# A four-layer sequence kernel on one core: the second layer's norm, skip term, convolution and gate products placed at other steps and on other engines

## The reference, cut to what matters

```python
h = _layernorm(x) * scale1 + shift1                  # per sequence, from cond
xz = h @ in_proj_W;  x_, z = split(xz)               # 512 channels each
x_ = silu(causal_conv(x_, conv_w, 4 taps) + conv_b)
xdbl = x_ @ x_proj_W                                 # rank-16 dt, B and C of 32 states
dt = softplus(xdbl[:16] @ dt_proj_W + dt_proj_b)
def step(hst, inp):                                  # over the 64 tokens, for 32 states
    hst = hst * exp(dt_t * A) + dt_t * B_t * x_t
    return hst, (hst * C_t).sum(states)
y = (ys + Dp * x_) * silu(z) @ out_proj_W            # all of this from h: once forwards,
x = x + gate1 * (y_forwards + y_backwards)           # once over the tokens in reverse
x = x + gate2 * (silu(h2 @ w1) * (h2 @ w2)) @ w3      # h2: the second norm; 384 hidden
```

## Time and profile before

| | us |
|---|---|
| median of 3 runs | 4816.87 |
| lowest and highest | 4813.54, 4817.01 |
| the profiled execution's own time | 4812.7 |
| its span | 4810.9 |
| mean granted TensorE clock, share of full | 0.976 |

### The profile page before, as it was taken

One profiled execution on the slowest core, in us unless ns is written; L12 is line 12 of the kernel. 1 busy time (PEld: TensorE's weight loads), 2 busy tenths in 40 slices (PEclk: granted clock), 3 DMA queues, 4 the chain that ended last, 5 costly groups with the idle time before them and its releaser, 6 DMA issues.

```text
span 4810.9 us, 83433 instructions
## 1 busy us (share of the span) xinstructions
PE 4498.8 (94%) x32892; PEld 3735.8 (78%) x32892; DVE 4162.1 (87%) x4023; ACT 4139.1 (86%) x6894; POOL 3991.3 (83%) x1064
## 2 busy tenths in 40 slices
PE   7989989899899998999999999999999999999998
PEld 5447878788778874458888888888888888888886
DVE  6658988999989976659999998999998998998996
ACT  3449899899899974459999999999999999999995
POOL 4429899889889984538999998998988999989995
PEclk8989999999999998999999999999999999999999
DMA  3001111111111111011121211211211211111111
GB/s 122 1 10 50 49 45 50 49 46 45 50 45 49 51 65 38 1 38 50 54 79 49 79 53 49 79 53 49 79 50 50 80 54 63 64 53 59 58 58 36
DMA packets 89813, 252.74 MB, mean 53 GB/s; under 512 B 12224, under 2 KB 25920, under 8 KB 89424
## 3 DMA queue, kind: packets, MB, share of 16 engines
q1 hardware_dynamic: 89424, 247.40, 14.8%
HBM read 243.70 MB, written 3.67 MB: 51 GB/s over the span
## 4 chain that ended last, share of the span: by engine, by line
PE 42%; ACT 29%; POOL 12%; DVE 9%; issue 7%; DVEq 0%; DMA 0%; POOLq 0%; SPq 0%; ACTq 0%
PE psum L895 11%; PE psum L701 9%; ACT weights_c L1399 9%; PE psum L881 8%; POOL work L2099 6%; PE psum L878 6%; ACT weights_c L1414 5%; PE psum L991 5%; ACT work L1399 4%; ACT work L1414 4%; POOL weights_c L2099 4%; DVE work L1764 3%; PE psum L1067 1%; DVE weights_c L1764 1%; ACT L1190 1%
## 5 line engine op out<-in xcount | busy, mean ns | idle before, releaser
L2099 POOL TENSOR_TENSOR work<-work,weights_a 128x2048 f32<-128x2048 f32 x512 | 2330.7, 4572 | 271.8 <-DVE work L1764 271.1
L1764 DVE TENSOR_TENSOR_SCAN work<-weights_c,psum 128x512 f32<-128x512 f32 x1366 | 1571.6, 1202 | 127.4 <-PE psum L881 118.1
L895 PE MATMUL psum<-ident,work 128*128 128x128 f32 x8192 | 1244.9, 276 | 20.2 <-POOL work L2099 19.8
L2099 POOL TENSOR_TENSOR weights_c<-weights_c,weights_a 128x2048 f32<-128x2048 f32 x256 | 1166.8, 4574 | 87.4 <-DVE weights_c L1764 87.0
L1399 ACT ACTIVATE work<-work,decay 128x504 f32<-128x504 f32 x1366 | 963.9, 706 | 63.8 <-DVE work L1764 30.4
L895 PEld LDWEIGHTS psum<-ident,work 128*128 128x128 f32 x8192 | 973.3, 143 | 28.7 <-POOL work L2099 27.8
L881 PE MATMUL psum<-ident,work 128*128 128x128 f32 x5464 | 941.2, 275 | 0.0
L1764 DVE TENSOR_TENSOR_SCAN weights_c<-work,psum 128x512 f32<-128x512 f32 x684 | 794.6, 1202 | 51.6 <-PE psum L881 44.3
L1764 DVE TENSOR_TENSOR_SCAN work<-work,psum 128x512 f32<-128x512 f32 x682 | 791.1, 1201 | 48.6 <-PE psum L881 42.2
L881 PE MATMUL psum<-ident,weights_c 128*128 128x128 f32 x3752 | 697.9, 276 | 0.0
L881 PEld LDWEIGHTS psum<-ident,work 128*128 128x128 f32 x5464 | 675.5, 143 | 0.0
(11 more groups left out here) (173 smaller groups left out, 6546.8 us busy)
## 6 DMA issues: line engine op xcount, KB each, us to landing
weights_a<-c_rows SPq DMA_DIRECT2D x384, 512.0 KB, 3.6
weights_c<-in_L_cond_fwd_in_w SPq DMA_DIRECT2D x8, 512.0 KB, 7.0
weights_c<-in_L_cond_fwd_xproj_w SPq DMA_DIRECT2D x4, 1024.0 KB, 7.7
weights_c<-in_L_cond_bwd_in_w SPq DMA_DIRECT2D x8, 512.0 KB, 5.9
weights_c<-in_L_cond_bwd_xproj_w SPq DMA_DIRECT2D x4, 1024.0 KB, 7.8
x_stream<-in_x_t SPq DMA_DIRECT2D x4, 512.0 KB, 8.7
weights_a<-in_L_cond_w SPq DMA_DIRECT2D x2, 1024.0 KB, 15.0
weights_a<-in_L_cond_W SPq DMA_DIRECT2D x2, 1024.0 KB, 8.3
```

The costliest lines, as they stand in the source:

```text
L895: last = nc.tensor.matmul(PS[:, t, j * P:(j + 1) * P], buf["ring"][s % RING][:, j, t * P:(t + 1) * P], IDENT[:, :], start=begins, stop=((s ...
L1764: v.tensor_tensor_scan(buf["ring"][s % RING][:, j, along], buf["decay"][q % DECAYS][:, along], PS[:, 4 + q % LOOKAHEAD, along], 0.0, ALU.mult,
L2099: g.tensor_tensor(state, state, buf["c"][:, s // 2 % 2, s % 2, :].unsqueeze(1).broadcast_to([P, DC, T]), ALU.mult).then_inc(ss["prod_ready ...
```

## The change

- **Norm.** The first norm of the next block moves from the odd run to the end of the even run before it (`next_mean` at 81, `next_var` at 90 in runs 2 and 4; 63 and 78 in run 0), with its seven operations on DVE, ACT and POOL.
- **Skip.** The odd run's `skip` becomes `later0` and `later1` at the end of the even run's POOL stream, and `add_skip` of an odd run stands at steps 1 to 4 (`skip_steps`).
- **Input and convolution.** `in` starts at step 3 of the odd run: at 3, 14, 25 and 36 in runs 3 and 5, with a `gate` job between each two, and at 3, 12, 22 and 32 in run 1 and in "run -1". The first taps are done by ACT (`tap`: a Copy with a scale from a vector, 512 columns, and one of 8 columns); DVE does the six others one after each of six steps.
- **z.** In the even run the four `z` jobs come ahead of `bc` (39 to 54; in run 0 from step 3), DVE copies them, and their Silu shares one pair of table loads with `silu_x`, which moves from step 25 to 60 (26 in run 0).
- The other jobs move accordingly: `bc` 63, `dt` 68 to 78 in runs 2 and 4 (71 to 81 in run 6), `bc` 49, `up` 55 to 63, `dt` 67 to 77, `down` 80 and 85 in runs 3 and 5. `dt` jobs have a gap of 3 in place of 4. `bt` and `dtx` end at 106 in all.

The core of the diff:

```diff
-        jobs += [("mean", KC, 3 if gated or tail and head else 10)]
+    if tail or r == RUNS - 1:
+        jobs += [("mean", KC, 3 if head else 10)]
+    if 0 <= r < RUNS - 1 and r % 2 == 0:
+        jobs += [(f"z{j}", KC, 3) for j in range(DC - 1)] + ([("var", KC, 3)] if tail else []) + [("z3", KC, 9)]
...
+    if first:
+        for j in range(DC):
+            jobs += [(f"in{j}", KC, 14 if j == DC - 1 else 7)] + ([(f"gate{j}", KC, 3)] if mlp and j < HIDDEN1 else [])
+        jobs += [("bc", DC, 3)]
...
+        jobs += [(f"dt{j}", 1, 3) for j in range(DC)]
+    if prepares1(r):
+        jobs += [("next_mean", KC, 10), ("next_var", KC, 3)]
...
+def prepares1(r):
+
+    return r % 2 == 0 and 0 <= r < RUNS - 2
...
-PIPES = {1: Pipe(32, 2, pipe_jobs1, lambda r: 2 if r % 2 else 12 if r >= 2 else 28),
+PIPES = {1: Pipe(32, 2, pipe_jobs1, lambda r: 3 if r % 2 else 12 if r >= 2 else 3),
...
+def skip_steps(l, r):
+
+    return (1, 2, 3, 4) if l == 1 and r % 2 else (17, 19, 21, 23)
...
+                    made("pool", f"later{j // 2}@{r - 1}" if l == 1 and r % 2 else f"skip{j // 2}@{r}")
...
+                            yield from product(f"in{j}", [by("dve", f"conv{j}_7"), by("act", f"tap{j}")],
+                                               chunk(W1["inp"], j), h, first(lambda: h_made(r)))
+                            if mlp and j < HIDDEN1:
+                                yield from gates(j)
...
+                    def tap(j):
+
+                        weight = VEC[:, VCONV + j * 4 + 3:VCONV + j * 4 + 4]
+                        yield plan.read(f"in{j}", 2)
+                        made("pe", f"in{j}@{r}")
+                        if r >= 0:
+                            act.wait_ge(ss["skip_added"], r + 1)
+                        f(XS1[:, j, :], bank[f"in{j}"], ACT.Copy, scale=weight)
+                        ends = [ap.rearrange("p (b s) -> p b s", s=SEQ)[:, :, SEQ - 1:SEQ]
+                                for ap in (XC1[:, j, :], bank[f"in{j}"])]
+                        f(ends[0], ends[1], ACT.Copy, scale=weight).then_inc(done(f"tap{j}"), 1)
...
+                    if even:
+                        yield max(plan.read("z3", 5), 26)
+                        made("dve", f"z3@{r}")
                         act.wait_ge(ss["skip_added"], r + 1)
+                        tables(SILU)
+                        f(Z1, Z1, ACT.Silu).then_inc(done("silu_z"), 1)
+                        silu_x(XC1)
+                        tables(EXP_LN)
+                        yield from low_rank()
...
+                    for n, i in enumerate((3, 2, 4, 5, 6, 7)):
+                        shift, d = divmod(i, 2)
...
+                        yield plan.read(f"in{j}", 3 + n)
+                        if i == 3:
+                            made("act", f"tap{j}@{r}")
+                        else:
+                            made("dve", f"conv{j}_{3 if i in (2, 5) else i - 2}@{r}")
...
+                            v.tensor_copy(Z1[:, j, :], bank[f"z{j}"]).then_inc(done(f"z{j}"), 1)
...
+                    if prepares1(r):
+                        halfway = norm(r, plan, done, 2, H, r // 2 + 1, f"z3@{r}", None, "next_")
+                        yield next(halfway)
+                        at = next(halfway)
+                    if even:
+                        yield from skip(r + 1, done, "later", (plan.read("dt3", 15), plan.read("dt3", 19)))
+                    if prepares1(r):
+                        yield at
+                        yield from halfway
```

More of the change, by code:

```diff
@@ L117, in pipe_jobs1 @@
 def pipe_jobs1(r):
-    head, tail = r < RUNS - 1, r >= 2 and r % 2 == 0
-    first, gated = r % 2 == 1 and head, r >= 3 and r % 2 == 1 or r == RUNS
-    norms = tail or r % 2 == 1 and r > 0
+    head, tail, first, mlp = r < RUNS - 1, ends1(r), inputs1(r), gated1(r)
     jobs = []
@@ L227, in pipe_steps1 @@
             g += ["soft0", "product0", "soft1", "product1"]
-        if gated:
+        if prepares1(r):
+            a += ["next_square", "next_var", "next_rstd"]
+            v += ["next_mean", "next_normed"]
+            g += ["next_scaled"]
+        if even:
+            g += ["later0", "later1"]
+        if prepares1(r):
+            g += ["next_h"]
+        if mlp:
             v += ["down0", "end0", "down1", "end1"]
-        if 0 <= r and r % 2 == 0 and head:
-            a += [f"z{j}" for j in range(DC)] + ["silu_z"]
         if head:
@@ L786, in up, with gates @@
-                    def up():
+                    def gates(*chunks):
+                        for j in chunks:
+                            yield from product(f"gate{j}", [by("act", f"gate{j}")], chunk(WM1["w1"], j), h2,
+                                               first(lambda: made("pool", f"h@{r if r == RUNS else r - 1}")))
+                    if tails:
+                        yield from tail(r, product, turn, by, YT1(r), W1["out"])
+                    if tails or r == RUNS - 1:
+                        yield from mean(r, product, by, nb, first(lambda: made("dve", f"x1@{r}")) if tails else None)
@@ L807, in beside1 @@
                                                lambda k: made("dve", f"up{k}@{r}"))
-                    if 0 <= r and r % 2 == 0 and head:
-                        for j in range(DC):
-                            yield from product(f"z{j}", [by("act", f"z{j}")], chunk(W1["inp"], DC + j), h)
                     if head:
@@ L1318, in beside1 @@
                             f(SOFT1[:, two, :], SOFT1[:, two, :], ACT.Ln, bias=ONEC[:, 0:1]).then_inc(done(f"ln{i}"), 1)
[L1319 to L1326 removed]
+                    if prepares1(r):
+                        yield from square(r, plan, done, "next_")
+                        yield from deviation(r, plan, bank["next_var"], done, "next_")
                     if head:
```

345 lines of the change are left out of this document (163 added, 182 removed).

## The result

**The change made the kernel slower, by 0.7%:** 4847.5 us, the median of 6 executions (4845.3 to 4848.3), against 4813.9 for the kernel before, measured beside it (6 executions, 4812.3 to 4817.0). The ratio is 1.0068, with a 95% interval from 1.0055 to 1.0081. The forecast was 4791. The profiled execution of after took 4845.3 us, its span 4843.6.

A forecast was written before the change was run, and what follows sets the result against it. No single engine bounds the kernel: a run costs the sum over its stretches of each one's slowest engine. Terms -1+1-7+5-13+4-13+0-1 = -25 on 4816.87 give about 4792, stated as 4791; own range 4775 to 4808, wider range 4758 to 4818.

The forecast's parts named there:

- Even runs, PE and DVE, steps 0 to 80: Run 2 to step 80, with six jobs crowding steps 39 to 60: 112 us against 108.4 before, +3.
- the clock's dips: Granted clock may dip elsewhere than before: at most a few us, counted within the range.
- POOL, steps 80 to 128: Even runs' end: POOL's late queue sets the pace, step 128 at 65.8 us against 62.7 before, +3.
- run 0: Second layer's first even run: +1 us, its POOL work falling between steps 56 and 88.
- Odd runs, steps 0 to 45: Runs 3 and 5: 65.1 us of DVE work, 3.2 for tap waits and 1.5 more, together 69.8.
- The start at step 3: Odd runs: `in` waits for nothing new; its first `tap` was given the common wait of 0.8 us.
- The gates: Runs 3 and 5: `gate` jobs claim bank 7 before the last tap and hold PE, 0.3 us each.
- The taps: Convolving runs: DVE waits for ACT's `tap`, 0.8 us a chunk, 3.2 a run.
- Behind step 45: Runs 3 and 5, steps 45 to 128: 112 us, from the old last stretch and 8 more steps.
- Run 1: 66.5 us to step 42 and 112.4 behind it: 179 against 186.2, -7.
- (c): Rival, runs 1, 3 and 5: every tap costs 5.7 us in place of 0.8, total +34, 4851; chance 0.09.
- (b): Rival, even runs' steps 80 to 128: POOL's full cost, 5.4 us more each, total -3, 4814; chance 0.15.

The follow-up runs named there:

- e2: Changed kernel with `silu_x` of runs 2, 4 and 6 back at step 25 with its own table loads: 4840.5 us.
- e7: Changed kernel with even runs in the order of the kernel before, only the next norm and later skip added: 4828.6 us.
- e5: Changed kernel with `later0` and `later1` on 8 of 512 columns, leaving out most of the later skip term: 4836.9 us.
- e6: As e5, with `next_scaled` and `next_h` on 8 of 512 columns too: 4841.7 us.
- e11: Changed kernel, odd runs only: `in` from step 5, gap before each gate 9 instead of 7, `up` jobs ahead of `bc`: 4838.0 us.
- e3: Changed kernel with the first taps back on DVE, ahead of the second in the same step: 4847.3 us.
- e15: As e14, with DVE's `next_normed` one step later: 4791.0 us, ratio to the kernel before 0.9958.
- e14: Edits of e10 and e11 together, plus DVE's six taps of each chunk one step later and the gap to the gate 10: 4796.9 us.
- e13: Edits of e10 and e11 together, plus the four first taps of runs -1, 1, 3 and 5 back on DVE: 4801.3 us.
- e10: As e7, with `next_mean` ahead of the `z` jobs, `next_var` behind them, and `later0` and `later1` at steps 104 and 112: 4816.8 us.

## Why the prediction was wrong

**Even runs, PE and DVE, steps 0 to 80: the first step that failed** ("52+31+29 = 112: +3"). Run 2 took 120.3 us to step 80, not 112, against 108.4 in the earlier trace rows. I added each stretch's engine time and drew ACT's lead from it, but the jobs depend on each other: `bc` waits for Silu (PE 2.4 us at step 66), `dt` for `bc`'s copy and DVE for ACT's Abs (1.8 at step 79), while six decays, three banks and in-order streams cover only a few steps. e2 gave back 5.6 us of this in three runs; e7, which restores the order, gave back all of run 6 and 2.5 us more. Of the whole miss of 57 us, 38 lie in the even runs. The forecast allowed for the clock's dips as a few us that fall anywhere; here they follow PE's waits, and may be up to half of what runs 2, 4 and 6 lost (estimate in the first section).

**POOL, steps 80 to 128.** The sum was near, 66.8 us in run 2, where I had 65.8, and that is partly luck, since it left out the clock (0.92 here) and the wait was elsewhere than expected. I priced products that are late for `add_up`; what happened was DVE waiting at `next_normed` and, in run 6, PE 4.9 us at `dtx0` for `multiply`. For **run 0** the term was +1 and the measured one +6.0. There POOL's work was all of it (e5, e6), in waits of PE for products, 8.6 us against 0.3 before. "Its POOL work falls between steps 56 and 88" was nearly so (58 to 95) and hid nothing.

**Odd runs, steps 0 to 45: the second step that failed** (69.8 us; measured 79.5 in run 3 and 77.6 in run 5, whose clock was higher). Three terms were mis-sized. The start at step 3: `tap` waited for `add_skip` on PE and DVE for `tap`, 3.2 us, where I had a common 0.8. The gates: I took 0.3 each, although the row I cited for it had shown 2.4; two of three held PE for 2.8 and 2.9 us, and "three are already issued and DVE has its taps to do meanwhile" covered little, since the taps end just when the gate gets its bank. The taps: the ten waits other than the two at the start were 0.9 to 1.4 us against 0.8, a small error. In run 3 the three come to 2.4, 5.9 and 0.5 us beyond the forecast and the clock to about 1.9, together 10.7 where 9.7 are missing. With start, gap and the place of `up` mended, e11 took 67.4 us. It has 18 taps there and not 24; the sum redone for 18 gives 50.0+11.3+2.4+1.5 = 65.2, and the three waits for `tap` were 5.2 us where it has 2.4. So the sum, with PE's pieces hidden beside DVE's taps, is near for that placement, which is not the one in the diff. Behind step 45 I had 112 and got 114.9 in run 3 and 113.4 in run 5; `up0` behind `bc`'s copy made one step 5.9 us long (4.4 in run 5). **Run 1**, which has no gates, came within 1.4 us of its term: 68.4 us to step 42 against 66.5, and 112.2 behind it against 112.4.

**The rivals.** (c) forecast 4851 from the taps and the result was 4847.5, but for another reason: the mean wait was 1.4 us, below its own threshold of 2.9, and taking the taps from ACT (e3) gained nothing clear of the spread. (b), POOL takes it back, was right for run 0 alone. The rival that happened, jobs crowded so that each waits for the one before, had no place in the list. Of the signs that the prediction named for being wrong, two came: odd runs above 190 us, and even runs longer by more than 10. The two table loads an even run came as forecast, at 1283 ns each, and run 7 moved by 0.6 us. The start of run 0, 4.9 us earlier, can't be credited to the change (last section).

**What stays.** e15's runs 2 and 4 are still 6 to 7 us above before's and run 0 is 6.6. In run 0 that is POOL's added work (e5, e6); for runs 2 and 4 I take it to be the next norm and the later skip term, in runs whose ACT was full already and whose POOL was nearly so the earlier trace rows, which no run shows. Whether the norm would do better in the odd runs, with the new order of the rest, was not tried.

## What to carry to other kernels

A sum of busy times by stretch gives the best case of a placement. Whether a given placement reaches it is read by walking each chain of dependent jobs (claim of a shared bank, copy-out, next product) through the in-order streams, with the distance in steps between each operation and its first use. Moving operations or their users by one or two steps, with one job's place, was worth 7.5 to 9.2 us a run here (e11), one step more 3.7 (e14), and changing the engine of the taps at most 1.8 (e13). Sharing table loads gained nothing here, since the jobs that follow came to stand directly behind the merged block. And stretches of two kernels up to the same step are compared only once their work has been counted.

## What the runs showed of the hardware

The same instructions take different times by the granted clock. Steps 24 to 32 and 56 to 64 of runs 3 and 5 of after are the same work, and yet (the first two rows are run 3's):

```profile
927.58:943.13 15.55, 14.90 (x93) 12.11 (x94) 11.26 (x12) 10.99 (x20) 9.11 (x3) 0.89 0.11 35
982.24:997.94 15.70, 13.10 (x83) 10.40 (x82) 10.53 (x10) 14.92 (x27) 9.50 (x3) 0.89 0.10 33
1309.24:1323.11 13.87, 13.22 (x93) 10.95 (x94) 11.26 (x12) 10.98 (x20) 9.12 (x3) 1.00 0.11 39
1362.02:1376.26 14.24, 11.65 (x83) 9.50 (x82) 10.52 (x10) 14.24 (x26) 9.48 (x3) 1.00 0.12 38
```

Both stretches hold a PE wait of 2.6 to 2.8 us in either run. In run 3 part of the time around the wait's end was granted at the lower level; run 5 kept the full clock in these two. A granted 0.89 in place of 1.00 cost 1.7 and 1.5 us, which is nearly the whole difference of 3.4 us between the two runs. In the first layer the mean clock over 80 to 120 us was 0.84 in after and 0.96 in e10, whose instructions up to there are the same, and run 0 began at 347.9 and 341.7 us. In e11, whose instructions up to there are also the same, it began at 351.4 us. So the whole time of a single execution says nothing of effects under some 10 us, unless it is read run by run.

ACT's first tap (run 3 of after) takes a little less than DVE's (run 3 of e13) for the 512 columns from PSUM, 688 ns against 750, and more for the 8 columns, 265 against 223. The Trainium skill, page "VectorE: DVE Perf Modes", section "Specifications", places ScalarE closer to PSUM and VectorE closer to SBUF. The wide operation is in line with that and the narrow one is not, and no run here separates where an engine sits from how fast it works. For the time the distance mattered more than the engine: 8.9 us in three runs (e14) against 4.0 (e13).
